# The layer norm of a windowed attention: means and moments per image on TensorE, subtraction on VectorE, matmuls of a half step in order of tile form

## The reference, cut to what matters

```
def _ln_c(x, g, b):
    mu = jnp.mean(x, axis=1, keepdims=True)
    var = jnp.mean((x - mu) ** 2, axis=1, keepdims=True)
    return (x - mu) * jax.lax.rsqrt(var + 1e-05) * g[:, None, None] + b[:, None, None]

y = _conv1x1(_ln_c(x, n1g, n1b), qkv_w, qkv_b)        # 192 -> 3 * 192 channels
cols = _unfold(y, WS, STRIDE, PAD)                    # windows of 8x8 at stride 6
q = win[:, :, :HEADS] * temp[None, None]
```

## Time and profile before

| what | value |
|---|---|
| median of three runs | 5882.74 us |
| lowest and highest | 5879.74 and 5885.18 us |
| span of the profiled execution | 5874.6 us |
| time around the span, against the median | 8.1 us |
| PE busy | 5234.5 us (89%) |
| DVE busy | 4111.9 us (70%) |
| ACT busy | 2823.1 us (48%) |
| POOL busy | 805.7 us (14%) |
| the stage of the change | 2169.65 to 2513.15 us of the span |

### The profile page before, as it was taken

The page is one execution under the profiler, slowest core; times in us unless marked ns, Lnnn a source line. Parts: engine busy times, 40 slices in busy tenths (PEclk is TensorE's granted clock), DMA queues, the critical chain, the costliest instruction groups (busy, mean ns, idle before and its releaser), DMA issues. The chain is left out here.

```text
span 5874.6 us, 85825 instructions
## 1 busy us (share of the span) xinstructions
PE 5234.5 (89%) x34692; PEld 2383.9 (41%) x34692; DVE 4111.9 (70%) x4899; ACT 2823.1 (48%) x3955; POOL 805.7 (14%) x826
## 2 busy tenths in 40 slices
PE   7799999999989989968869799989778888888879
PEld 2355555555544434445534333333233333333323
DVE  3477677776621122278878499959789999999963
ACT  1144444444432223245521455526587777867844
POOL 1000000000000011122243100000033333323300
PEclk9899999999999989989989899989889999999999
DMA  6522121221032223344433000013300000000034
GB/s 214 138 39 42 22 42 23 40 43 22 15 110 70 81 77 129 111 142 142 132 119 123 29 29 29 33 47 113 99 29 29 5 28 25 16 29 5 17 113 164
DMA packets 298982, 398.22 MB, mean 68 GB/s; under 512 B 143916, under 2 KB 281316, under 8 KB 295324
## 3 DMA queue, kind: packets, MB, share of 16 engines
q1 hardware_dynamic: 271452, 302.90, 17.6%
q0 software_dynamic: 16096, 73.39, 3.7%
q10 hardware_dynamic: 11040, 16.43, 0.9%
HBM read 226.16 MB, written 166.49 MB: 67 GB/s over the span
## 5 line engine op out<-in xcount | busy, mean ns | idle before, releaser
L3884 DVE TENSOR_TENSOR_SCAN s_h<-s_da,s_h 128x448 f32<-128x448 f32 x672 | 729.6, 1124 | 1.5 <-ACT s_da L3811 1.4
L3731 PE MATMUL s_py<-s_prod,s_idf 128*128 128x448 f32 x1344 | 586.6, 559 | 24.5 <-ACT s_ycol L3824 23.3
L622 PE MATMUL b_pc<-b_ca,b_wdm 128*113 128x392 f32 x1152 | 486.9, 520 | 31.9 <-DVE b_wdm L837 25.8
L3811 ACT ACTIVATE s_da<-s_dt,s_al 128x448 f32<-128x448 f32 x672 | 406.1, 658 | 198.3 <-DVE s_h L3884 147.6
L765 ACT ACTIVATE b_band<-b_psel 124x784 f32<-124x784 f32 x264 | 217.7, 825 | 427.5 <-PE b_psel L690 424.4
L622 PE MATMUL b_pc<-b_cb,b_wdm 128*113 128x392 f32 x960 | 403.0, 520 | 0.0
L3869 DVE TENSOR_TENSOR s_h<-s_dtu,s_pb 128x896 f32<-128x896 f32 x336 | 354.9, 1056 | 31.7 <-POOL s_dtu L3918 23.2
L3891 DVE TENSOR_TENSOR s_prod<-s_h,s_pc 128x896 f32<-128x896 f32 x336 | 360.8, 1074 | 0.1
L3907 POOL TENSOR_TENSOR s_dt<-s_dt,s_dtu 128x448 f32<-128x448 f32 x168 | 249.3, 1484 | 782.7 <-DVE s_h L3884 427.5
L2861 DVE SCALAR_TENSOR_TENSOR j_zc<-j_zt,kept_vec,j_zc 128x896 f32<-128x896 f32 x320 | 344.9, 1144 | 6.7 <-ACT j_zt L2803 6.4
L3731 PEld LDWEIGHTS s_py<-s_prod,s_idf 128*128 128x128 f32 x1344 | 249.2, 193 | 220.0 <-issue 167.3
(11 more groups left out here) (726 smaller groups left out, 11252.0 us busy)
## 6 DMA issues: line engine op xcount, KB each, us to landing
b_qk<-mid_qkvp SPq DMA_DIRECT2D x96, 240.2 KB
d_vt<-mid_vd SPq DMA_DIRECT2D x200, 96.0 KB
d_qs<-mid_qd SPq DMA_DIRECT2D x20, 744.0 KB, 5.3
d_ks<-mid_kd SPq DMA_DIRECT2D x20, 744.0 KB, 7.7
b_v<-mid_qkvp SPq DMA_DIRECT2D x6, 1922.0 KB
mid_pout<-d_out POOLq DMA_DIRECT2D x20, 558.0 KB, 4.4
mid_qkvp<-a_out SPq DMA_DIRECT2D x42, 248.0 KB, 2.2
mid_qkvp<-a_out ACTq DMA_DIRECT2D x42, 248.0 KB, 2.1
```

Source lines behind the costliest of these rows:

```text
L622: mm = pe.matmul(pc[n % 2][0:113, 0:392], wdm[:, slot, p, 0:113], src, start=(w == STARTS[a]), stop=(w + 1 == STARTS[a + 1]))
L3731: mm = pe.matmul(y, idf[:, :], prod[j % 3][:, e, :], start=(pr == 0 and e == 0), stop=False)
L3811: last = a.activation(da[j % 4][:, e, :], dt[s % 2][:, span(c)], ACT.Exp, scale=al[:, u, n:n + 1])
L3884: v.tensor_tensor_scan(x, along(da[j % 4][:, e, :]), x, before_, ALU.mult, ALU.add).then_inc(scanned, 1)
```

## The change

TensorE no longer forms the centred values. It forms only the negative mean of each image, spread over 128 partitions, in two banks of q_pa (one for each image), and VectorE computes gate * x + (-mean) into `ce` with four instructions, one each for the two halves of block 1 and for blocks 0 and 2. The moment is likewise formed for each image alone. `rs` has two blocks instead of three, and the multiplication into `xn` is three instructions. ScalarE squares `ce` from SBUF in two parts, evacuates two of three q blocks and all three k blocks; VectorE evacuates one q block, and no k. The matmuls of a half step are issued by form: all pairs, then all full ones, then the halves. The matrices `gk`, `keep` and `m192h` are gone.

```
-            def centre(s):
...
-                pe.matmul(pA[:, 0, 0:CH], gk[:, q, 0, :], inner(s, 0), start=True, stop=False)
-                pe.matmul(pA[:, 1, 0:CH], gk[:, q, 1, :], inner(s, 1), start=True, stop=False)
-                pe.matmul(pA[:, 2, 0:CH], gk[:, q, 2, :], inner(s, 2), start=True, stop=False)
-                pe.matmul(pA[:, 0, 0:CH], gd[lo, q, 1, :], inner(s, 1, lo), start=False, stop=True)
-                pe.matmul(pA[:, 2, 0:CH], gd[hi, q, 1, :], inner(s, 1, hi), start=False, stop=True)
-                pe.matmul(pA[lo, 1, 0:CH], gd[:, q, 0, lo], inner(s, 0), start=False, stop=True)
-                pe.matmul(pA[hi, 1, 0:CH], gd[:, q, 2, hi], inner(s, 2), start=False, stop=True).then_inc(centred, 1)
+            def mean_pair(s):
...
+                    pe.wait_ge(log_done, s)
+                pe.matmul(pA[:, 0, 0:CH], gd[lo, q, 1, :], inner(s, 1, lo), start=True, stop=False)
+                pe.matmul(pA[:, 1, 0:CH], gd[hi, q, 1, :], inner(s, 1, hi), start=True, stop=False)
+            def mean_full(s):
+                q = s // NCH
+                pe.matmul(pA[:, 0, 0:CH], gd[:, q, 0, :], inner(s, 0), start=False, stop=True).then_inc(centred, 1)
+                pe.matmul(pA[:, 1, 0:CH], gd[:, q, 2, :], inner(s, 2), start=False, stop=True).then_inc(centred, 1)
+            def moment_pair(s):
+                pe.wait_ge(copied, 4 * s + 4)
+                pe.wait_ge(squared, 2 * s + 1)
+                pe.matmul(pA[:, 0, 0:CH], m192[lo, :], sq[lo, 1, :], start=True, stop=False)
+                pe.matmul(pA[:, 1, 0:CH], m192[hi, :], sq[hi, 1, :], start=True, stop=False)
+            def moment_full(s):
+                pe.wait_ge(squared, 2 * s + 2)
+                pe.matmul(pA[:, 0, 0:CH], m192[:, :], sq[:, 0, :], start=False, stop=True)
+                pe.matmul(pA[:, 1, 0:CH], m192[:, :], sq[:, 2, :], start=False, stop=True).then_inc(spread, 1)
+            def project_pair(s, m):
...
+                    pe.wait_ge(normed, 3 * s + 2)
+                    if s:
+                        pe.wait_ge(k_evac, 3 * s - 1)
+                else:
+                    pe.wait_ge(q_evac_v, s + 1)
+                    pe.wait_ge(q_evac_a, 2 * s + 1)
+                pe.matmul(pB[0][:, 0, 0:CH], w[lo, 1, base:base + 128], x[lo, 1, :], start=True, stop=False)
+                pe.matmul(pB[2][:, 0, 0:CH], w[hi, 1, base + 64:base + 192], x[hi, 1, :], start=True, stop=False)
+            def project_full(s, m):
...
+            def project_halves(s, m):
...
+            def values_pair(s, i):
...
+            def values_full(s, i):
...
             for s in range(NS2 + 1):
...
+                for m in range(2):
+                    if s < NS2:
+                        (mean_pair, moment_pair)[m](s)
+                    if s:
+                        project_pair(s - 1, m)
+                        values_pair(s - 1, m)
+                    if s < NS2:
+                        (mean_full, moment_full)[m](s)
+                    if s:
+                        values_full(s - 1, m)
+                        project_full(s - 1, m)
+                        project_halves(s - 1, m)
...
             def square(s):
...
-                a.activation(ce[s % 2][:, :, :], pA[:, :, 0:CH], ACT.Copy).then_inc(copied, 1)
-                a.activation(sq[:, :, :], pA[:, :, 0:CH], ACT.Square).then_inc(squared, 1)
+                a.wait_ge(copied, 4 * s + 2)
+                a.activation(sq[:, 1, :], ce[s % 2][:, 1, :], ACT.Square).then_inc(squared, 1)
+                a.wait_ge(copied, 4 * s + 4)
+                a.activation(sq[:, 0:3:2, :], ce[s % 2][:, 0:3:2, :], ACT.Square).then_inc(squared, 1)
...
+            def centre(s):
+                x, m, g = xs[s % NX], ce[s % 2], gt[:, s // NCH, :]
+                if s >= 2:
+                    v.wait_ge(squared, 2 * (s - 1))
+                for i, (t, p, image) in enumerate(((1, lo, 0), (1, hi, 1), (0, slice(0, 128), 0), (2, slice(0, 128), 1))):
+                    if i < 2:
+                        v.wait_ge(centred, 2 * s + i + 1)
+                    v.scalar_tensor_tensor(m[p, t, :].rearrange("p (h w) -> p h w", w=W), x[p, t, :, 3:3 + W], g[p, t:t + 1],
+                                           pA[p, image, 0:CH].rearrange("p (h w) -> p h w", w=W), ALU.mult, ALU.add).then_inc(copied, 1)
...
-                v.tensor_tensor(xn[s % 2][:, :, :], ce[s % 2][:, :, :], rs[:, :, :], ALU.mult).then_inc(normed, 1)
+                v.tensor_tensor(x[lo, 1, :], m[lo, 1, :], rs[lo, 0, :], ALU.mult).then_inc(normed, 1)
+                v.tensor_tensor(x[hi, 1, :], m[hi, 1, :], rs[hi, 1, :], ALU.mult).then_inc(normed, 1)
+                v.tensor_tensor(x[:, 0:3:2, :], m[:, 0:3:2, :], rs[:, :, :], ALU.mult).then_inc(normed, 1)
```

More of the change, by code:

```diff
@@ L1785, in project, with pixels @@
                         pe.wait_ge(folded, 6)
[L1786 removed]
+                    pe.wait_ge(normed, 3 * s + 2)
[7 more added lines that the diff above has]
+            def project_full(s, m):
+                x, base = xn[s % 2], C * m
+                pe.matmul(pB[0][:, 0, 0:CH], w[:, 0, base:base + 128], x[:, 0, :], start=False, stop=True).then_inc(product, 1)
+                pe.matmul(pB[2][:, 0, 0:CH], w[:, 2, base + 64:base + 192], x[:, 2, :], start=False, stop=True).then_inc(product, 1)
+                if m == 0 and s:
                     pe.wait_ge(k_evac, 3 * s)
[L1788 to L1790 removed]
+                if m == 1:
+                    pe.wait_ge(q_evac_a, 2 * s + 2)
                 pe.matmul(pB[1][:, 0, 0:CH], wd[:, m, :], x[:, 1, :], start=True, stop=False)
[L1792 to L1794 removed]
+            def project_halves(s, m):
+                x, base = xn[s % 2], C * m
                 pe.matmul(pB[1][lo, 0, 0:CH], w[:, 0, base + 128:base + 192], x[:, 0, :], start=False, stop=True)
                 pe.matmul(pB[1][hi, 0, 0:CH], w[:, 2, base:base + 64], x[:, 2, :], start=False, stop=True).then_inc(product, 1)
[L1798 removed]
+            def pixels(i, j):
+                return slice(112 * (2 * i + j), 112 * (2 * i + j) + 112)
+            def values_pair(s, i):
                 x, n = xn[s % 2], 2 * s + i
@@ L1803, in values @@
                 for j in range(2):
-                    px = slice(112 * (2 * i + j), 112 * (2 * i + j) + 112)
                     out = slice(C * j, C * j + C)
-                    pe.matmul(pV[0:112, 0, out], x[:, 0, px], w[:, 0, 2 * C:3 * C], start=True, stop=False)
-                    pe.matmul(pV[0:112, 1, out], x[:, 2, px], w[:, 2, 2 * C:3 * C], start=True, stop=False)
-                    pe.matmul(pV[0:112, 0, out], x[lo, 1, px], w[lo, 1, 2 * C:3 * C], start=False, stop=True)
-                    mm = pe.matmul(pV[0:112, 1, out], x[hi, 1, px], w[hi, 1, 2 * C:3 * C], start=False, stop=True)
+                    pe.matmul(pV[0:112, 0, out], x[lo, 1, pixels(i, j)], w[lo, 1, 2 * C:3 * C], start=(j == 0), stop=False)
+                    pe.matmul(pV[0:112, 1, out], x[hi, 1, pixels(i, j)], w[hi, 1, 2 * C:3 * C], start=(j == 0), stop=False)
+            def values_full(s, i):
+                x = xn[s % 2]
+                if i == 0:
+                    pe.wait_ge(normed, 3 * s + 3)
+                for j in range(2):
+                    out = slice(C * j, C * j + C)
+                    pe.matmul(pV[0:112, 0, out], x[:, 0, pixels(i, j)], w[:, 0, 2 * C:3 * C], start=False, stop=(j == 1))
+                    mm = pe.matmul(pV[0:112, 1, out], x[:, 2, pixels(i, j)], w[:, 2, 2 * C:3 * C], start=False, stop=(j == 1))
                 mm.then_inc(v_done, 1)
             for s in range(NS2 + 1):
-                if s < NS2:
-                    centre(s)
-                if s:
-                    project(s - 1, 0)
-                    values(s - 1, 0)
-                if s < NS2:
-                    moment(s)
-                if s:
-                    project(s - 1, 1)
-                    values(s - 1, 1)
+                for m in range(2):
[10 more added lines that the diff above has]
+                        project_halves(s - 1, m)
         @block.scalar
@@ L1924, in _ @@
             for s in range(NS2 + 1):
+                if s < NS2:
+                    centre(s)
                 if s:
+                    if s == 1:
+                        v.wait_ge(cleared, 4)
+                        v.wait_ge(bias_ready, 1)
                     values(s - 1, 0)
+                    queries(s - 1)
+                    values(s - 1, 1)
                 if s < NS2:
                     normal(s)
-                if s:
-                    keys(s - 1)
-                    values(s - 1, 1)
 def window_strips(nc, qd, kd, vd, biasT, proj_wT, proj_b, ident, pout):
```

84 lines of the change are left out of this document (31 added, 53 removed).

## The result

The changed kernel takes 5800.35 us (median of four runs, 5794.87 to 5803.89) against 5882.04 us for the kernel before (four runs, 5879.74 to 5885.18). The ratio is 0.986, with a 95% interval of 0.9846 to 0.9874: 81.7 us less, where 77.6 less (5805 us) was forecast. The profiled execution took 5794.87 us with a span of 5792.9.

What follows compares the result with a forecast made beforehand. PE (TensorE), busy without a pause, was taken to bound the stage. 13 steps x 5.70 = 74.1 us, plus 3.5 at the start, plus 1.5 and minus 1.5 at the end, made 77.6 less: 5805 us, range 5796 to 5820.

Steps and rivals of the forecast that it cites:

- PE bounds the stage: Mid-stage, PE's own stream sets the time: busy 21.00 of 21 us, VectorE 5.25, ScalarE 5.75.
- The step: PE's repeating step in the stage: from 22.70 to 17.00 us, 5.70 less, 74.1 us over 13 steps.
- Its two parts: Within a step on PE: 2.99 us from four removed matmul times, 2.69 from 14 removed changes of form.
- The forms join: PE's grouped matmuls: successive pairs, and 128 beside 112 stationary columns, cost no change of form; 0 us taken for both.
- Rival 2: PE's groups: three seams a half step still cost 0.1925 us each, 16 us in all: 5821 us; chance 5%.
- The chains have slack: VectorE and ScalarE results reach PE 1.6 us or more ahead; 2.4 spare before the moment's pair, 1.6 before k's.
- Rival 1: A wait on VectorE's queue delays PE by 1 us in one or both half steps: 5819 to 5833 us; chance 7%.
- The start: Stage start up to the second step: 3.5 us less, 1.9 if the clock rises only after the moment.
- The end: Stage end: last two half steps 1.5 us less, V's stores behind k's 0.4 for issue and 1.1 for data more.
- Rival 3: PE pauses drop the granted clock to 1.2 GHz: 5911 us for half the stage, 6014 for all; chance 2%.

Runs made afterwards that it cites:

- experiment 3: Changed kernel with fewer matmuls kept, but each call's matmuls in the old order: step 20.08 us against 17.08, median 5849.33 us, ratio 0.9944.
- experiment 2: Kernel before with its seven centre and seven moment matmuls kept on TensorE but issued by form: step 20.98 us against 22.70, median 5861.69 us, ratio 0.9967.
- experiment 5: Changed kernel with a bank of its own for k's block 1, its halves beside q's: step 16.92 us against 17.08, single run 5809.41 us.
- Experiment 6: Changed kernel with the first mean between the bias sums, or three unread products in the start's gap: starts 19.90 and 21.69 us against 23.3 to 26.2.

## Why the prediction was right, point by point

- **PE bounds the stage, and goes on doing so.** Right: 21.00 of 21 us before and after, with VectorE 1.9 and ScalarE 1.7 times as busy. Nothing was given back in the steady state.
- **The step.** Forecast 17.00 us, measured 17.08. The 0.08 lies in the V matmuls (four in 1.30 us, 0.325 each, for which I had 0.32) and in rounding of the changes. 13 x 5.62 = 73.1 us less instead of 74.1.
- **Its two parts.** Forecast 2.69 from 14 changes of form and 2.99 from four matmul times. Both are shown apart: 12 changes cost 2.35 us (0.196 each, experiment 3), ten are worth 1.72 (0.17, experiment 2), one 0.16 (experiment 5). From the grouped-only kernel to the changed one four matmul times and four changes go, 20.98 - 17.08 = 3.90 against 2.99 + 0.77 forecast.
- **The forms join.** Right, read from PE's timeline: no seam between pairs of different calls or between 128 and 112 columns. Rival 2 is out. By the rule that the prediction weighed (the Trainium skill, "TensorE: Matmul & The Clock Gate", "Part 3: Packing small matmuls": a load overlaps only where the row groups differ) pairs in a row would have bought less; the trace of after doesn't bear it out, with 0.37 to 0.38 us from pass to pass where the pairs of 448 columns follow one another.
- **The chains have slack.** Right, and measured by making the chain 2.4 us longer: 2.3 and 1.6 us spare where 2.4 and 1.6 were forecast. Rival 1 is out, and it was close enough to be real: at 2.4 us more it costs 0.92 us a step. The forecast had half-partition products at 0.52 and they take 0.61, and it had the DMA share at 0.59 where 0.48 was measured; nobody waited for either.
- **The start.** The term of the forecast that was mis-sized: -3.5 forecast (-1.9 if the clock rises only after the moment), measured -2.7, +0.2 and -0.1 in three executions of the changed kernel. That the first comes near is in part luck, as two errors cancel in it. Ahead of the first mean pass 9.45 us instead of 10.86 (2178.92 - 2169.47 against 2180.51 - 2169.65), in all three executions: -1.4 where I had taken -0.4. From there to the second step, with that step's excess, it is 13.9 us where my sum had 12.1. The wait for xn that makes the excess was in the sum (1.35; the excess is 1.52); what was missing is that the moment ran for the most part at the lower clock, although the clock had risen in the mean: the second step begins 12.3 us behind the first mean and not 10.8. In the two repeats the low clock takes another 2.9 and 2.6 us. Experiment 6 shows that a start with the clock held up is 1.6 us shorter than the best of the three; what takes the clock down is not shown. I had also read a single wait of PE for another engine in the order before; the earlier trace rows have a second one, 1.48 us at the second step's opening, which changes no term of the sum.
- **The end.** The last half steps -1.5 and the stores +1.5 forecast, net 0; measured 22.38 us before (2490.77 to 2513.15) and 22.43 after (2414.76 to 2437.19). Both parts are right as well: V's store is issued 14.31 us into it instead of 15.37 (-1.06, with -1.5 + 0.4 forecast), and from there it takes 8.12 instead of 7.01 (+1.11, with +1.1 forecast).
- **Rival 3, the clock.** In the steady stage PEclk is 1.00. The lower level appears only in the stage's start, before and after, and at the end of experiment 3.
- **What the forecast did not contain.** The profiled execution after had 2.0 us around its span, not 8.1; if that holds for the one before, it was some 5 us quicker than its median. That cost nothing, as the profile after was as much below its own. And a stage without any change was 5.2 us shorter in the first pair of profiles. That is chance of the execution: beside the kernel before, the changed one was measured three times, and the medians differ by 81.7, 73.1 and 77.3 us, 77.3 on the average, with 77.6 forecast. The changed stage alone is 75.8, 72.8 and 73.2 us shorter in its three profiles, which is 2 to 5 less than forecast: 1.0 of it by the step, the rest by the start's term. So the mechanism is right, and that totals agree to a microsecond is chance.

What stays open: why the granted clock of the next stage is 0.90 in one execution and 0.93 in another, and what takes the start's clock down and brings it back at once in some executions and 10 us later in others. Neither was pursued.

## What to carry to other kernels

Where TensorE is without a pause, count changes of tile form like matmuls: here each costs 0.16 to 0.2 us, a quarter of a full 448-column f32 product, and the 14 changes fewer (12 by the order, 2 with the dropped products) removed nearly as much as dropping four products did. Order the groups so that what needs the first part of an operand stands ahead of what needs the last; the same order then gives the other engines their slack, and doubling a suspected instruction measures how much of it there is. Compare the changed stage's own length in the trace before believing a difference of totals of a few microseconds: a stage that nobody touched moved by 19 us between executions.

## What the runs showed of the hardware that I had not expected

- TensorE's granted clock had risen to 2.4 GHz and was back at 1.2 GHz behind an idle gap of 2.5 us in the changed kernel, and stayed at 2.4 GHz through one of 2.66 us in the kernel before. Products without a reader in the gap (2.42 us of them, one execution) made the second step start 1.6 us earlier.
- A scalar_tensor_tensor with one PSUM operand takes 0.68 us on 64 partitions as on 128, and the same instruction twice in a row starts every 0.6 us.
- The same next stage, with the same 12080 PE rows, took 483.6 to 502.3 us in twelve profiles, with a granted clock of 0.93 to 0.90.
